# Second MLP matmul and inverse transform channel-major, image added at the eviction, first attention normalisation folded into weights

## The reference, cut to what matters

```
# layer 0
h = depthwise_conv7x7(x) + conv_b
h = layernorm(h) * ln_g + ln_b                    # over the 96 channels of a token
h = gelu(h @ w1 + b1)                             # 96 -> 384
t1 = x + (h @ w2 + b2) * layer_scale              # 384 -> 96
# layer 1, attention-like block
z = relu(bn1(layernorm(t1) @ aw1.T))              # 96 -> 192
X = fft(z, over tokens)
y = ifft(relu(X.re*r - X.im*i + rb) + 1j*relu(X.im*r + X.re*i + ib)).real
t2 = t1 + bn2(y @ aw2.T)                          # 192 -> 96
# layer 1, feed-forward block in rounded formats (fp8 e5m2 factors, fp16 sums)
out = t2 + q(relu(q(layernorm(t2) @ W1.T + b1)) @ W2.T + b2)
```

## Time and profile before

| what | value |
|---|---|
| median of 3 runs | 4698.79 us (4695.02 to 4704.4) |
| the profiled execution, its own time | 4703.32 us |
| its span, first to last instruction | 4701.3 us |
| mean granted TensorE clock | 0.955 |
| busy: PE, DVE, ACT, POOL | 4316.8, 3481.5, 2557.6, 1408.7 us |
| one pass of the steady loop (from x load to x load) | 123.35 us |
| DMA, mean over the span | 114 GB/s |

### The profile page before, as it was taken

How to read it: one execution, slowest core, us unless ns; L and a number is a source line. 1 busy time by engine, 2 the same in 40 slices (tenths; PEclk the granted TensorE clock), 3 DMA queues, 4 the chain that set the end, 5 groups by cost and what they waited for, 6 DMA issues and landing times.

```text
span 4701.3 us, 100572 instructions
## 1 busy us (share of the span) xinstructions
PE 4316.8 (92%) x28624; PEld 3532.8 (75%) x28624; DVE 3481.5 (74%) x13109; ACT 2557.6 (54%) x5282; POOL 1408.7 (30%) x1060
## 2 busy tenths in 40 slices
PE   4999969999999999999999999999999999999986
PEld 2444438888888888888888888888888888888874
DVE  1333335788888888888888888888888888888877
ACT  2343325565565655555556655555565565565653
POOL 1111153333333333333333333333333233333321
PEclk7999979999999999999999999999999999999996
DMA  5666623444444444444333434344444444444331
GB/s 137 170 170 170 170 85 91 109 111 116 113 113 111 116 111 116 113 111 115 100 100 105 110 103 108 105 112 111 114 111 115 113 115 111 113 115 111 105 90 51
DMA packets 427312, 536.67 MB, mean 114 GB/s; under 512 B 219591, under 2 KB 385131, under 8 KB 411051
## 3 DMA queue, kind: packets, MB, share of 16 engines
q1 hardware_dynamic: 412558, 510.37, 40.2%
q10 hardware_dynamic: 14272, 20.04, 1.7%
HBM read 295.17 MB, written 235.12 MB: 113 GB/s over the span
## 4 chain that ended last, share of the span: by engine, by line
PE 78%; issue 4%; DVE 2%; DMA 1%; ACT 1%; POOL 0%; SPq 0%; POOLq 0%; DVEq 0%; ACTq 0%
PE psum L974 12%; PE psum L987 11%; PE psum L984 8%; PE psum L1030 7%; PE psum L1021 7%; PE psum L1010 6%; PE psum L1002 6%; PE psum L1044 4%; PE psum L1037 3%; PE psum L1066 3%; PE psum L1059 3%; PE psum L994 2%; PE psum L967 2%; PE psum L1051 2%; PE psum L1070 2%
## 5 line engine op out<-in xcount | busy, mean ns | idle before, releaser
L683 POOL TENSOR_TENSOR sums<-sums,minus_half 112x4 f32<-112x4 f32 (+1 forms) x480 | 631.0, 1318 | 2127.4 <-DVE sums L829 2127.4
L703 POOL TENSOR_SCALAR minus<-minus 96x448 f32<-96x448 f32 (+1 forms) x512 | 640.9, 1252 | 640.9 <-DVE minus L868 619.0
L974 PE MATMUL psum<-hn,w_sb 96*128 96x448 f32 x1344 | 613.4, 597 | 162.0 <-issue 160.2
L987 PE MATMUL psum<-w_sb,hid 128*112 128x96 f32 x5376 | 679.6, 263 | 0.0
L987 PEld LDWEIGHTS psum<-w_sb,hid 128*112 128x112 f32 x5376 | 617.6, 181 | 0.0
L744 ACT ACTIVATE hid<-psum,b_sb 128x448 f32<-128x448 f32 x672 | 418.1, 637 | 336.9 <-PE psum L974 298.6
L974 PEld LDWEIGHTS psum<-hn,w_sb 96*128 96x128 f32 x1344 | 262.8, 208 | 364.4 <-issue 354.0
L386 PE MATMUL c_psum<-c_xt,c_toeplitz 128*112 128x448 f32 x1152 | 479.3, 554 | 48.9 <-ACT c_xt L328 23.1
L834 DVE TENSOR_SCALAR xn<-t,sums 112x96 f32<-112x96 f32 x1792 | 514.4, 349 | 7.4 <-POOL sums L683 7.4
L414 DVE TENSOR_SCALAR c_h<-c_psum,c_bias 112x448 f32<-112x448 f32 x192 | 199.0, 1037 | 430.1 <-PE c_psum L386 430.1
L984 PE MATMUL psum<-skip,x_sb 97*112 97x96 f32 x1792 | 503.7, 363 | 2.4 <-ACT hid L744 2.4
(11 more groups left out here) (82 smaller groups left out, 7471.4 us busy)
## 6 DMA issues: line engine op xcount, KB each, us to landing
outer_spectrum<-outer SPq DMA_DIRECT2D x448, 168.0 KB
inner<-outer_spectrum SPq DMA_DIRECT2D x32, 2016.0 KB
c_xpad<-x SPq DMA_DIRECT2D x96, 392.0 KB, 11.2
h_tokens<-c_h SPq DMA_DIRECT2D x24, 1568.0 KB, 8.3
h<-h_tokens SPq DMA_DIRECT2D x32, 1176.0 KB, 13.2
x_sb<-x SPq DMA_DIRECT2D x32, 1176.0 KB, 8.0
residual_stream<-t SPq DMA_DIRECT2D x224, 168.0 KB, 2.1
inner_inverse<-unmixed SPq DMA_DIRECT2D x224, 168.0 KB, 2.4
```

The costliest lines, as they stand in the source:

```text
L683: nc.gpsimd.tensor_tensor(su[:, :, 6], su[:, :, 5], minus_half[:, 0:su.shape[1]], ALU.pow).then_inc(ready.sem, 1)
L703: nc.gpsimd.tensor_scalar(part, part, 0.0, None, ALU.max).then_inc(clipped.sem, 1)
L974: pe.matmul(bank("M1", c, m, CW, 128), w1_sb[:, m * 128:(m + 1) * 128], hn[:, c * CW:(c + 1) * CW], start=True, stop=True).then_inc(m1_mad ...
L987: last = pe.matmul(dst[:, j * C:(j + 1) * C], hid[:, c % 2, m, j * PT:(j + 1) * PT], w2_sb[:, m, :], start=False, stop=(m == KF - 1))
```

## The change

M2 becomes three matmuls of 448 columns with `w2_sb` as weights and `hid` as the moving side. Its result has channels on partitions (96 x 448). VectorE, not ScalarE, empties it, with the bias `b2_sb` and the image added in the same instruction; the image is read at a step of 28 elements. t1 lies channel-major in SBUF and in DRAM. `skip` and N go. T now transposes t1 to tokens on partitions, and VectorE takes statistics from that PSUM bank. W1 multiplies t1 itself with weights from which the mean over channels has been taken out (`centre`), and VectorE multiplies by the tile's 1/deviation and takes the maximum with `below`, minus the batch norm's shift; the shift itself is a row of act1 (partition 112) and a row of the outer transform. ScalarE's copy of T and its relu of W1 go.

AP has `back` as weights and gives channels on partitions; the add of t1 is channel-major. A new step S2 transposes t2 to tokens on partitions, ScalarE copies it to t2_rows, and from that VectorE takes statistics and N2 normalises. F2's transposes of t2 go; the last add reads t2 directly. The chain of small operations has five steps instead of six, and POOL writes its powers into a tile of their own. The rings are four banks for ScalarE, two for VectorE (M2, T, W1, AP). Positions of T, AP, S2, N2 and T2 are new. The setup of the constants changes.

```diff
 STAGES = {
-    1: {"M1": (-3, 11.8, NC), "M2": (7, 11.8, NC), "N": (15, 11.8, NC), "T": (19, 11.8, NC),
-        "W1": (22, 11.8, NC), "A": (27, 11.8, NC)},
+    1: {"M1": (-3, 11.8, NC), "M2": (7, 11.8, NC), "T": (13, 11.8, NC), "W1": (22, 11.8, NC), "A": (27, 11.8, NC)},
...
-    3: {"AP": (6, 11.5, NC), "N2": (12, 11.5, NC), "T2": (17, 11.5, NC), "F1": (20.5, 12, NC),
+    3: {"AP": (3, 11.5, NC), "S2": (8, 11.5, NC), "N2": (14, 11.5, NC), "T2": (18, 11.5, NC), "F1": (20.5, 12, NC),
...
-    "dve": {"B": 3, "M2": 2, "F2": 2, "AP": 1, "L0N": -1, "W": -2},
-    "pool": {"B": 4, "M2": 3, "AP": 2, "N2": -2, "F1": 1},
-    "sp": {"T": 2, "W1": -0.5},
+    "dve": {"B": 3, "M2": 2, "T": 2, "W1": 1, "F2": 2, "AP": 1, "S2": 1, "L0N": -1, "W": -2},
+    "pool": {"B": 4, "T": 3, "S2": 2, "F1": 1},
+    "sp": {"M2": 3},
...
-RING = {"act": 5, "dve": 1, "spec": 2}
+RING = {"act": 4, "dve": 2, "spec": 2}
...
 # chain of statistics, VectorE
-                nc.vector.tensor_scalar(su[:, :, 3], su[:, :, 0], 0.5, None, ALU.mult)
-                nc.vector.tensor_tensor(su[:, :, 4], su[:, :, 2], su[:, :, 2], ALU.mult)
-                nc.vector.tensor_scalar(su[:, :, 5], su[:, :, 1], 4.0 / C, 4 * eps, ALU.mult, ALU.add
-                                        ).then_inc(step.sem, 1)
+                nc.vector.scalar_tensor_tensor(out=su[:, :, 4], in0=su[:, :, 2], scalar=C / 4.0, in1=su[:, :, 2],
+                                               op0=ALU.mult, op1=ALU.mult)
+                nc.vector.tensor_scalar(su[:, :, 3], su[:, :, 0], 0.5, None, ALU.mult).then_inc(step.sem, 1)
                 dve.wait_ge(step.sem, step.at(n, 3 * c + 2))
-                nc.vector.tensor_tensor(su[:, :, 5], su[:, :, 5], su[:, :, 4], ALU.add).then_inc(seen.sem, 1)
+                nc.vector.scalar_tensor_tensor(out=su[:, :, 5], in0=su[:, :, 1], scalar=C * eps, in1=su[:, :, 4],
+                                               op0=ALU.add, op1=ALU.add).then_inc(seen.sem, 1)
...
 # M2, T and W1 on VectorE
+                        dve.wait_ge(m2_made.sem, m2_made.at(n, c))
...
+                        nc.vector.scalar_tensor_tensor(
+                            out=t1[:, c % 4, :].rearrange("c (q p) -> c q p", q=CH),
+                            in0=bank("M2", c, 0, CW, C).rearrange("c (q p) -> c q p", q=CH), scalar=b2_sb[:, 0:1],
+                            in1=x_sb[:, :].rearrange("c (p q) -> c q p", q=NQ)[:, part, :], op0=ALU.add, op1=ALU.add
+                            ).then_inc(t1_done.sem, 1)
+                    if name == "T":
+                        dve.wait_ge(rows1_made.sem, rows1_made.at(n, c))
+                        see(1, bank("T", c, 0, CH * C, PT).rearrange("p (t c) -> p t c", t=CH), 0
+                            ).then_inc(ln_step[1].sem, 1)
...
+                            for k in range(2):
+                                at = CH * (c % 2) + 2 * m + k
+                                last = nc.vector.scalar_tensor_tensor(
+                                    out=act1[0:PT, j % 4, k, :], in0=z[:, k * H2:(k + 1) * H2],
+                                    scalar=scales[1][:, at:at + 1], in1=below[:, :], op0=ALU.mult, op1=ALU.max)
...
 # M2, AP and S2 on TensorE
-                        for j in range(CH):
-                            q = CH * c + j
-
-                            pe.matmul(dst[:, j * C:(j + 1) * C], x_sb[:, q:q + (PT - 1) * NQ + 1:NQ], skip[:, :],
-                                      start=True, stop=False)
-                            for m in range(KF):
-                                last = pe.matmul(dst[:, j * C:(j + 1) * C], hid[:, c % 2, m, j * PT:(j + 1) * PT],
-                                                 w2_sb[:, m, :], start=False, stop=(m == KF - 1))
+                        for m in range(KF):
+                            last = pe.matmul(dst, w2_sb[:, m, :], hid[:, c % 2, m, :], start=(m == 0), stop=(m == KF - 1))
...
-                            last = pe.matmul(dst[:, j * C:(j + 1) * C], outer_inv[:, CH * c + j, :],
-                                             back[:, CH * c + j, :], start=True, stop=True)
+                            last = pe.matmul(dst[:, j * PT:(j + 1) * PT], back[:, CH * c + j, :],
+                                             outer_inv[:, CH * c + j, :], start=True, stop=True)
...
+                    if name == "S2":
+                        dst = bank("S2", c, 0, CH * C, PT)
+                        pe.wait_ge(t2_done.sem, t2_done.at(n, c))
+                        for j in range(CH):
+                            last = pe.transpose(dst[:, j * C:(j + 1) * C], t2[:, c % 4, j * PT:(j + 1) * PT], ident[0:C, 0:C])
...
-                        for j in range(CH):
-                            last = pe.transpose(dst[:, j * PT:(j + 1) * PT], t2[:, c % 4, j, :], ident[0:PT, 0:PT])
-                        last.then_inc(t2t_made.sem, 1)
```

More of the change, by code:

```diff
@@ L476, in image_phase @@
         stats = [sb(f"stats{n}", [PT, NQ if n == 0 else CH, 6]) for n in range(3)]
-        sums = [sb(f"sums{n}", [PT, NQ if n == 0 else CH, 7]) for n in range(3)]
+        sums = [sb(f"sums{n}", [PT, NQ if n == 0 else CH, 6]) for n in range(3)]
+        scales = [sb(f"scales{n}", [PT, NQ if n == 0 else 2 * CH]) for n in range(3)]
         psum = ctx.enter_context(nc.psum_tensor("psum", [128, 8, 512], F32))
@@ L528, in image_phase @@
         t2_done = signal("t2_done", NC, first=2)
+        rows2_made = signal("rows2_made", NC, first=2)
+        rows2_done = signal("rows2_done", NC, first=2)
         ln2_seen = signal("ln2_seen", NC, first=2)
@@ L582, in turns @@
             turn("end", NB + 1)
-        constant_rows(nc, wts, x_sb, xnt, inner, back)
+        constant_rows(nc, wts, inner, back, act1, psum)
         credit_all(nc, signals)
@@ L679, in _, with deviation @@
         def _(pool):
-            def deviation(which, ready):
+            def deviation(which, c, ready):
                 su = sums[which]
-                nc.gpsimd.tensor_tensor(su[:, :, 6], su[:, :, 5], minus_half[:, 0:su.shape[1]], ALU.pow
+                w = su.shape[1]
+                at = w * (c % 2)
+                nc.gpsimd.tensor_tensor(scales[which][:, at:at + w], su[:, :, 5], minus_half[:, 0:w], ALU.pow
                                         ).then_inc(ready.sem, 1)
@@ L745, in turn @@
                                                  bias=b1_sb[:, m:m + 1]).then_inc(gelu_done.sem, 1)
[L746 to L751, removed]
-                    if name == "W1":
-                        for m in range(2):
-                            j = 2 * c + m
-                            act.wait_ge(a1_made.sem, a1_made.at(n, j))
-                            act.wait_ge(outer_made.sem, outer_made.at(*before(n, j, 2 * NC, 4)))
-                            nc.scalar.activation(act1[:, j % 4, :, :].rearrange("p t h -> p (t h)"),
-                                                 bank("W1", c, m, 2 * H2, PT), ACT.Relu).then_inc(act1_done.sem, 1)
                     if name == "A":
@@ L786, in turn @@
                         nc.scalar.copy(mixed[:, c % 2, 0:w], bank("W", c, 0, w, PT)).then_inc(mixed_done.sem, 1)
+                    if name == "S2":
+                        act.wait_ge(rows2_made.sem, rows2_made.at(n, c))
+                        act.wait_ge(xn2_done.sem, xn2_done.at(*before(n, c, NC, 2)))
+                        nc.scalar.copy(t2_rows[:, c % 2, :, :].rearrange("p t c -> p (t c)"),
+                                       bank("S2", c, 0, CH * C, PT)).then_inc(rows2_done.sem, 1)
                     if name == "T2":
@@ L1000, in turn @@
                             for j in range(2):
                                 at = (2 * m + j) * PT
[L1002 removed]
+                                last = pe.matmul(dst[:, j * H2:(j + 1) * H2], t1[:, c % 4, at:at + PT],
                                                  aw1_sb[:, :], start=True, stop=True)
@@ L1091, in _ @@
         def _(dve):
-            nc.vector.memset(x_sb[C:C + 1, :], 1.0)
-            nc.vector.memset(xnt[C:C + 1, :, :], 1.0)
+            nc.vector.memset(constant, 0.0).then_inc(rows_set, 1)
+            dve.wait_ge(rows_set, 1)
+            nc.vector.memset(constant.rearrange("o (q m) -> o q m", m=2 * K1)[:, :, 0:1], PT / NTOK ** 0.5).then_inc(rows_set, 1)
+            dve.wait_ge(centred, 1)
+            nc.vector.tensor_copy(wts.aw1[:, :], psum[0:C, 0, 0:H2])
+        @block.tensor
+        def _(pe):
+            pe.matmul(psum[0:C, 0, 0:H2], wts.centre[:, :], wts.aw1[:, :], start=True, stop=True).then_inc(centred, 1)
 def hn_tiles(hn, c):
@@ L1124, in __init__ @@
         self.w2 = sb("w2_sb", [128, KF, C])
-        self.skip = sb("skip", [C + 1, C])
-        self.aw1 = sb("aw1_sb", [C + 1, H2])
+        self.b2 = sb("b2_sb", [C, 1])
+        self.aw1 = sb("aw1_sb", [C, H2])
+        self.centre = sb("centre", [C, C])
+        self.below = sb("below", [PT, H2])
+        self.shift1 = sb("shift1", [1, H2])
         self.aw2 = sb("aw2_sb", [C, 2, C])
```

(2 more changed lines are left out.)

177 lines of the change are left out of this document (94 added, 83 removed).

## The result

The changed kernel takes 4889.07 us (median of 4 runs, 4882.35 to 4893.08) against 4700.57 for the kernel before on the same chip: ratio 1.0407, 95% interval 1.0394 to 1.042. It is slower by 4%, with 12% fewer instructions in the trace and TensorE busy 86% of the span, where it was 92%. Of all executions here one, the second of run e1, took 8678.72 us, nearly twice the others; it isn't explained and is left out of e1's figures.

The account below looks back on a forecast made before the run. The bound was to move from TensorE to VectorE: 110.0 us work, 17.6 waits and 1.4 handovers make a 129.0 us turn, +5.65. 4703.3 + 29 x 5.65 - 20 = 4847, less 4.5 gives 4843 us; range 4600 to 4965.

Parts of the forecast that it names:

- The forecast's own sign of being wrong: Listed signs against the forecast included a VectorE wait at the loop's end below 8 us a turn.
- TensorE's work: Second MLP matmul: 11.7 us a turn less; TensorE busy about 106 us of a 129 us turn.
- VectorE's work: VectorE's busy time in a steady turn: from 102.65 to 110.0 us, +7.4 us (5.8 to 8.5).
- The image eviction: VectorE emptying M2 with the image read at a step: 0.83 us each, +5.8 us a turn (4.2 to 6.9).
- the +1.6 us: Stage 1 statistics reading PSUM instead of SBUF: +0.055 us each, 28 a turn, +1.6 us (0 to 1.6).
- The wait at the loop's end: VectorE's wait before the residual add, behind TensorE's standstill and slow restart: 9.4 us a turn would remain.
- The waits at the start: VectorE at the turn's start waiting for M2, S2's copy and uw: 1.6, 0.1 and 1.9, together 3.6 us.
- The new handovers: Coupling through the two PSUM banks shared by M2, T, W1 and AP: 1.4 us a turn, between 0 and 6.0.
- rival 3: Two-bank ring makes engines take turns, or TensorE's clock is lowered more often: 133.6 us a turn, 4976 us; chance 0.14.
- The mark that I had named for rival 3: VectorE itself waiting more than 4 us a turn for M2, T or W1 in mid-turn.
- Outside the loop's turns: Stretches "first" and "second": -20 us together; last three stages and setup: 0.
- The rival of a gain: VectorE's added waits cost nothing and its sum stays under 123.35: 120.6 us a turn, 4599 us; chance 0.23 including in-between outcomes.

Follow-up runs that it names:

- e1: Changed kernel with M2's eviction reading 448 neighbouring image elements instead of elements 28 apart (wrong tokens added): 4783.63 us, ratio 1.0184 to the kernel before.
- e2: Changed kernel with every M1 and M2 matmul of 448 columns issued as four of 112: 5207.62 us, ratio 1.1103 to the kernel before.
- e10: Kernel before with one of M2's three weight slices left out, 28 matmuls less in TensorE's loop: 4581.51 us, ratio 0.9757.
- e11: Kernel before with all three of M2's weight slices left out, only the matmul adding image and bias kept: 4363.20 us, ratio 0.9287.
- e7: Changed kernel with S2's statistics, POOL's power, N2 and T2 placed later in the written order: 4921.01 us, ratio 1.0479 to the kernel before.
- e9: Changed kernel with M2 2.3 units earlier in TensorE's order, ahead of T2 of the chunk before: 5093.20 us, ratio 1.0838 to the kernel before.
- e12: Order of e9 with three PSUM banks each for VectorE's and ScalarE's rings: 4842.97 us, ratio 1.0306 to the kernel before.
- e5: Changed kernel with W1 emptied by ScalarE instead of VectorE, batch norm's shift left out of the maximum: 4850.15 us, ratio 1.0328 to the kernel before.
- e3: Changed kernel with only M2's matmuls issued as two of 224 columns: 4894.22 us, ratio 1.0429 to the kernel before.

## Why the prediction was right or wrong

The direction, the size (4843 forecast, 4889 measured) and the turn (129.0, 129.83) came out. The forecast's own sign of being wrong, a wait at the loop's end below 8 us, was there too. That the bound leaves TensorE is shown; that VectorE's sum then sets the turn is only partly so, and the sum came out by two errors of opposite sign.

- TensorE's work. Three M2 matmuls took 2.26 us (2005.55 to 2007.81) against 2.29. But busy is 113.1 a turn, not 106. The clock of 0.93 is most of it: in e1, with the same TensorE work and 0.97, it is 108.6. The rest isn't explained.
- VectorE's work: 109.1 against 110.0. W1 0.327 us start to start, as forecast. The image eviction is 1.03 us long and holds VectorE 0.95, where I took 0.83: +0.8 a turn. The Trainium skill's rule that the prediction cites (SBUF — State Buffer, section "Door 1: The DMA port swizzle"), that each access which crosses to a new 16-byte line pays, agrees with the trace: in e1 the read costs 0.35 us less on 448 elements. Statistics from PSUM last 250 ns against 244, and four take 0.74 us from either: the +1.6 us was wrong, the +0.055 of L868 against L883 doesn't carry over to them, so here two errors cancel. The final add, 987 ns, gained nothing from SBUF.
- The wait at the loop's end: 9.4 forecast, 2.3 measured (17.9 us in 7.7 turns). This is the term that failed first. I read "issue" in the earlier trace rows as a property of the loop, and counted it as pinned. It was the loading of a loop body too long to be kept, and the change itself shortened the body: M2 has 3 matmuls a chunk instead of 16. e2, e10 and e11 show it.
- The waits at the start: 3.6 forecast, 1.3 + 1.9 = 3.2 measured.
- The new handovers: 1.4 forecast, some 10.3 measured (7.9 for S2's copy, 2.4 for W1), all in mid-turn. I priced the two-bank ring and left out of the sum that S2 stands behind T2 and M2 in TensorE's order, and what a wait does to the clock of the matmuls behind it (rival 3 names the clock, the sum does not). The timeline and e7 show the order, e9 against e12 the ring in the order of e9. The mark that I had named for rival 3, more than 4 us of VectorE's waits for M2, T or W1 in mid-turn, isn't reached: W1's is 2.4, and S2, which uses a bank of ScalarE, is not among the three. So the engines do take turns, 8.9 us a turn above my term for it, but mostly over S2 and T2 and not over the ring that rival 3 named. The price was hidden because the standstill went.
- These two against each other: 9.4 - 2.3 = 7.1 too much, 10.3 - 1.4 = 8.9 too little. That is luck: each alone is larger than the 5.65 us by which the turn was forecast to grow. Over all 28 turns, with the parts of the loop-end wait that the profile puts down to issue, they are 2.7 and 9.8, and the errors 6.7 and 8.4.
- Outside the loop's turns: from x load to x load "first" fell from 91.7 to 84.5 and "second" from 97.6 to 94.8, -10 where I had -20; the next stretch, up to the first load in the loop, rose from 116.8 to 132.4, +15.5 where I had one turn's 5.65; the part behind the last load in the loop went from 290.1 to 300.2 us where I had 0.
- The rival of a gain did not come: 4599 needed VectorE's sum under 123.35 and no waits.

Open: how much of the 10.3 us is the lower clock after a wait and how much the wait itself. In e1 a small relief brought the clock to 0.97 and more time than the work removed, in e5 a large one did neither (0.94); no run holds the clock fixed. The convolution phase, the same in both, ended some 16 us earlier in the profiled execution of after; that isn't explained.

## What to carry to other kernels

A "standstill by issue" at a loop's end can be a price of the loop body's length, as here, so look at the instruction queue's packets per turn before counting it as fixed: shortening the body below the limit can be worth more than the work saved (from e2 to after the turn falls by 10.9 us, TensorE's busy time by 6.1). Before work is moved from a full engine to one 83% busy, write down not only its new sum but, for each new handover, what stands in front of it in the in-order lists of both engines. With a ring of two banks, a step issued earlier can cost more than it gains; with a third bank the same order paid (e9, e12).

## What the runs showed of the hardware that was not expected

- TensorE's loop body is loaded again in each turn above some length, here between 696 and 780 matmul records with as many weight loads (e3, e10), and is kept below it: 5.7 us of standstill (4.5 in e2), then M1 at the lower level, 4.84 us instead of 2.3; VectorE, behind it, waited 10 us in place of 2.3.
- A 448-column fp32 matmul whose moving side has a step of 28 elements takes 1.61 us instead of 0.76; the same step costs a VectorE read 0.35 us on 448 elements.
- Statistics take as long from PSUM as from SBUF (250 and 244 ns).
